# Top-k attention in two streams: the longest rows paired with the shortest

## The reference, cut to what matters

```python
dots = jnp.einsum('bhid,bhjd->bhij', q, k) * SCALE          # keys: 16 memory + n tokens
dots = jnp.einsum('bhij,hk->bkij', dots, pre_proj)          # heads are mixed
dots = jnp.where(causal, mask_value, dots)
kth = jax.lax.top_k(dots, TOPK)[0][..., -1:]                # TOPK = 64
dots = jnp.where(dots < kth, mask_value, dots)
attn = jax.nn.softmax(dots, axis=-1)
out = jnp.einsum('bhij,bhjd->bhid', attn, v)
return out.transpose(0, 2, 1, 3).reshape(b, n, H * DH) @ Wout + bout
```

## Time and profile before

| | |
|---|---|
| median of 3 runs | 5859.57 us (5858.61 to 5865.69) |
| profiled execution | 5879.23 us |
| its span | 5877.4 us, 141554 instructions |
| PE, PEld busy | 4961.7 us (84%), 3162.0 us (54%) |
| DVE busy | 4472.4 us (76%) |
| ACT, POOL busy | 3359.7 us (57%), 2310.0 us (39%) |
| mean granted clock of PE | 0.902 |

### The profile page before, as it was taken

How to read it: one execution, slowest core, us unless ns; L and a number is a source line. 1 busy time by engine, 2 the same in 40 slices (tenths; PEclk the granted TensorE clock), 3 DMA queues, 4 the chain that set the end, 5 groups by cost and what they waited for, 6 DMA issues and landing times. The chain is left out here.

```text
span 5877.4 us, 141554 instructions
## 1 busy us (share of the span) xinstructions
PE 4961.7 (84%) x53142; PEld 3162.0 (54%) x53334; DVE 4472.4 (76%) x8591; ACT 3359.7 (57%) x7309; POOL 2310.0 (39%) x3182
## 2 busy tenths in 40 slices
PE   4775999999999997667667677575999999999997
PEld 1322666666666665334334344343666666666665
DVE  5996777676767674898997997995777777777774
ACT  2433777676767675334334334332777777777775
POOL 1222666665666663000000000001666666666663
PEclk6998999999999999776877887776999999999998
DMA  0001222222222221000000000000222222222221
GB/s 17 0 0 36 66 73 66 71 65 72 64 74 63 74 63 29 16 1 2 1 2 2 1 1 1 1 2 25 68 70 71 70 66 74 63 74 67 74 66 37
DMA packets 162565, 248.01 MB, mean 42 GB/s; under 512 B 36228, under 2 KB 56640, under 8 KB 161734
## 3 DMA queue, kind: packets, MB, share of 16 engines
q1 hardware_dynamic: 161862, 238.65, 15.5%
HBM read 36.15 MB, written 1.05 MB: 6 GB/s over the span
## 5 line engine op out<-in xcount | busy, mean ns | idle before, releaser
L929 POOL TENSOR_TENSOR f_rope<-f_rope,f_t 128x1024 f32<-128x1024 f32 x384 | 906.4, 2360 | 475.2 <-DVE f_t L843 475.2
L942 POOL TENSOR_TENSOR f_rope<-f_rope,f_rn 128x1024 f32<-128x1024 f32 x384 | 731.3, 1904 | 59.9 <-POOL f_rn L921 4.4
L479 PE MATMUL psum<-f_wqkv,f_xs 128*128 128x512 f32 x1536 | 734.3, 601 | 17.0 <-DVE f_t L843 17.0
L848 DVE TENSOR_REDUCE f_ss<-f_sq 128x16 f32<-128x1024 f32 x384 | 466.1, 1214 | 336.8 <-ACT f_sq L710 333.4
L1722 DVE MAX8 tk_m<-tk_work 128x8 f32<-128x408 f32 (+28 forms) x1624 | 678.1, 460 | 0.0
L1761 POOL TENSOR_TENSOR X<-tk_y,X 128x128 f32<-128x128 f32 x16 | 7.0, 436 | 1674.1 <-ACT tk_y L1667 1674.1
L1727 DVE MATCH_REPLACE8 tk_work<-tk_m,tk_work 128x408 f32<-128x408 f32 (+28 forms) x1392 | 623.6, 456 | 0.0
L673 ACT ACTIVATE f_kT<-psum 64x512 f32<-64x512 f32 (+1 forms) x960 | 485.6, 525 | 81.6 <-PE psum L470 72.1
L710 ACT ACTIVATE f_sq<-psum 128x1024 f32<-128x1024 f32 x384 | 393.3, 1024 | 223.8 <-PE psum L479 223.3
L865 DVE TENSOR_REDUCE f_den<-f_prob 128x16 f32<-128x1024 f32 x192 | 234.2, 1220 | 365.4 <-ACT f_prob L715 365.4
L551 PE MATMUL psum<-f_wqkv,f_xs 128*128 128x512 f32 x768 | 383.3, 623 | 110.4 <-DMA f_wqkv<-in_Wqkv 75.7
(11 more groups left out here) (237 smaller groups left out, 10054.2 us busy)
## 6 DMA issues: line engine op xcount, KB each, us to landing
f_v<-f_v_tok SPq DMA_DIRECT2D x1152, 128.0 KB, 2.4
f_v<-f_v_tok SPq DMA_DIRECT2D x768, 64.0 KB, 2.0
f_wqkv<-in_Wqkv SPq DMA_DIRECT2D x36, 512.0 KB, 5.3
f_wo<-in_Wo SPq DMA_DIRECT2D x12, 512.0 KB, 4.3
f_w<-in_W SPq DMA_DIRECT2D x12, 341.0 KB, 4.0
f_w<-in_W SPq DMA_DIRECT2D x24, 64.0 KB
tk_wkv<-in_Wkv SPq DMA_DIRECT2D x1, 1024.0 KB
out<-y_tok SPq DMA_DIRECT2D x4, 256.0 KB, 2.5
```

The lines of the kernel that those rows point to most:

```text
L479: last = pe.matmul(psum[:, n, :], xs[:, j % 2, :], wqkv[:, INNER * which + 512 * n:INNER * which + 512 * (n + 1)], start=True, stop=True)
L848: dve.tensor_reduce(ss[:, H * half:H * (half + 1)], sq[:, half, :, :], AX_X, ALU.add).then_inc(s[f"{name}_ss"], 1)
L929: pool.tensor_tensor(part, part, t2[:, half, :, :], ALU.add).then_inc(s[f"{name}_added"], 1)
L942: pool.tensor_tensor(part, part, rn[:, H * half:H * (half + 1)].unsqueeze(2).to_broadcast([P, H, DH]), ALU.mult).then_inc(s[f"{name}_norme ...
```

## The change: what it does

`place` now alternates two streams: unit j = 0 of a pair walks down from the longest rows of the sequence, unit j = 1 walks up from the shortest. A pair is (63 - i, i) for i = 0 to 31. Its two units have 552 keys together, always. Four pairs make a *quad*: 32 neighbouring queries of each stream, so a block of `weigh` for each. The unit j = 1 of the first six pairs has at most 64 keys and one round, while its partner has eight: the number of rounds is now kept for each unit, with counters `found` and `gone` for the semaphore values.

What was done per tile is now done per quad or per two. `project_q` makes the queries of one quad, 32 of each stream: 16 products with 32 moving columns into one bank, in the first slot of the quad before. `weigh` of the long stream stands in the second slot of the next quad, of the short stream in the third, `turn_output` in the third and fourth. `output` is made per 64 queries and stream (two products, one after the other in the first slot of every second quad), and POOL adds halves of a tile. Values of the next sequence are made in slots 3 (two tiles), 4 (one) of that sequence and 23 (one) of the one before, keys in slots 3, 11, 19 and 27. The transposed probabilities lie in two buffers, for up to 3 full tiles and for 1.

```diff
 def place(unit):
     b, rest = divmod(unit, UNITS)
-    pos, u = divmod(rest, UNITS // TILES)
-    return b, TILES - 1 - pos, u
+    i, j = divmod(rest, 2)
+    g = i if j else UNITS - 1 - i
+    t, u = divmod(g, P // QB)
+    return b, t, u
...
+def values_due(slot):
+    b, at = divmod(slot, 4 * QUADS)
+    if 0 < b < B and at in (3, 4):
+        return [(b, t) for t in ((0, 1) if at == 3 else (2,))]
+    return [(b + 1, 3)] if at == 23 and b + 1 < B else []
+def halves_due(slot):
+    quad, r = divmod(slot, 4)
+    if r or quad % 2 == 0 or quad < 3:
+        return []
+    return [((quad - 3) // 2, stream) for stream in range(2)]
+def keys_due(slot):
+    b, at = divmod(slot, 4 * QUADS)
+    return [(b + 1, at // 8)] if at % 8 == 3 and b + 1 < B else []
+def queries_due(slot):
+    return [slot // 4 + 1] if slot % 4 == 0 and slot // 4 + 1 < QUADS * B else []
...
-def project_q(T):
-    b, t = tile(T)
-    for n in range(2):
-        bank = side(("q", T, n))
-        for c in range(4):
-            w0 = 512 * n + P * c
-            last = pe.matmul(bank[:, P * c:P * (c + 1)], wq[:, w0:w0 + P], k.XA[:, b, PAD + P * t:PAD + P * (t + 1)], start=True, stop=True)
-        last.then_inc(s["side_full"], 1)
+def project_q(quad):
+    bank = side(("q", quad))
+    for stream in range(2):
+        b, q0 = queries(quad, stream)
+        for c in range(PAIRS):
+            at = BLOCK * (PAIRS * stream + c)
+            last = pe.matmul(bank[:, at:at + BLOCK], wq[:, P * c:P * (c + 1)], k.XA[:, b, PAD + q0:PAD + q0 + BLOCK], start=True, stop=True)
+    last.then_inc(s["side_full"], 1)
...
-def output(T):
-    bank = side(("y", T))
-    pe.wait_ge(s["ot_evac"], 1 + 4 * T + 4)
+def output(h, stream):
+    bank = side(("y", h, stream))
+    pe.wait_ge(s["ot_evac"], 1 + 4 * h + 4)
     for c in range(8):
-        last = pe.matmul(bank[:, 0:P], wout[:, c // 4, c % 4, :], oT[:, c, :], start=(c == 0), stop=(c == 7))
+        last = pe.matmul(bank[:, 0:HALF], wout[:, c // 4, c % 4, :], oT[:, stream, c, :], start=(c == 0), stop=(c == 7))
...
 for slot in range(SLOTS + 5):        # PE
+    quad, r = divmod(slot, 4)
+    finished = 0 <= quad - 1 < QUADS * B
     if slot + 1 < SLOTS:
         raw_dots(slot + 1)
     if 0 <= slot - 1 < SLOTS:
         turn(slot - 1)
     if slot + 1 < SLOTS:
         mix(slot + 1)
-    if slot % 2 == 1 and 0 <= (slot - 3) // 2 < SLOTS // 2:
-        weigh((slot - 3) // 2)
-    if slot % 2 == 0 and 0 <= (slot - 4) // 2 < SLOTS // 2:
-        turn_output((slot - 4) // 2)
+    if finished and r in (2, 3):
+        turn_output(2 * (quad - 1) + r - 2)
+    if finished and r in (1, 2):
+        weigh(quad - 1, r - 1)
+    # then values, halves, keys and queries that are due in this slot; ACT copies in the same order
...
 def pair(p, between):                # DVE
-    rounds = ROUNDS if selects(2 * p) else 1
-    for r in range(rounds):
+    rounds = [ROUNDS if selects(2 * p + j) else 1 for j in range(2)]
+    for r in range(ROUNDS):
         for j in range(2):
+            if r < rounds[j]:        # maximum of unit j
...
         for j in range(2):
+            if r < rounds[j] - 1:    # strike of unit j
...
         if r == 5:
             between()                # now in all slots; reciprocal in slots 1 and 2 of a quad
```

More of the change, by code:

```diff
@@ L1340, in side_uses @@
-        return {use: i for i, use in enumerate(uses)}
[L1342 to L1352, removed]
+        for slot in range(SLOTS + 5):
+            uses += [("v", b, t, n) for b, t in values_due(slot) for n in range(2)]
+            uses += [("y", h, stream) for h, stream in halves_due(slot)]
+            uses += [("k", b, t, n) for b, t in keys_due(slot) for n in range(2)]
+            uses += [("q", quad) for quad in queries_due(slot)]
@@ L1354, in topk_phase, with queries, half_start @@
+        return {use: i for i, use in enumerate(uses)}
     AT = side_uses()
-    FIRST = 2 + 2 * TILES + 2 * TILES
+    FIRST = 1 + 2 * TILES + 2 * TILES
     def side_bank(i):
         return (SIDE, OUT, TURN_DIAG, TURN)[i % 4] if i < FIRST else SIDE
+    def queries(quad, stream):
+        b, t, u = place(8 * quad + stream)
+        return b, P * t + BLOCK * (u // 4)
+    def half_start(h, stream):
+        return h // 4, HALF * (h % 4 if stream else 7 - h % 4)
     with ExitStack() as ctx:
@@ L1469, in raw_dots @@
                 def raw_dots(pair):
[L1471 to L1474, removed]
+                    quad = pair // 4
+                    if pair % 4 == 0:
+                        pe.wait_ge(s["side_evac"], 1 + (1 + 2 * TILES if quad == 0 else AT[("q", quad)] + 1))
                     for j in range(2):
                         unit = 2 * pair + j
-                        u = place(unit)[2]
+                        b, t, u = place(unit)
                         if unit >= 2:
@@ L1593, in side, with copy_q @@
                     return psum[:, side_bank(i), :]
-                def copy_q(T):
-                    for n in range(2):
-                        bank = side(("q", T, n)).rearrange("p (g r u i) -> p g r u i", g=2, r=2, i=QB)
+                def copy_q(quad):
+                    bank = side(("q", quad)).rearrange("p (s g r u i) -> p s g r u i", s=2, g=4, r=2, i=QB)
+                    for stream in range(2):
                         for r in range(2):
@@ L1656, in normalise, with copy_output, copy_y @@
                     last.then_inc(s["o_done"], 1)
[L1658 to L1667, removed]
+                def copy_output(quad, stream):
+                    act.wait_ge(s["ot_full"], 1 + 2 * quad + stream + 1)
+                    b, q0 = queries(quad, stream)
+                    at = q0 % HALF
+                    copy(oT[:, stream, :, at:at + BLOCK], psum[:, OUT, 0:2 * P].rearrange("p (c q) -> p c q", q=BLOCK)).then_inc(s["ot_evac"], 1)
+                def copy_y(h, stream):
+                    bank = side(("y", h, stream))
+                    if h:
+                        act.wait_ge(s["added"], 1 + 2 * h + stream - 1)
+                    act.activation(y[:, stream, :], bank[:, 0:HALF], ACT.Identity, bias=bout[:, 0:1]).then_inc(s["side_evac"], 1)
                 copy_q(0)
@@ L1676, in _ @@
                 for slot in range(SLOTS + 5):
-                    T, part = divmod(slot, TILE_PAIRS)
+                    quad, r = divmod(slot, 4)
+                    finished = 0 <= quad - 1 < QUADS * B
                     if slot + 1 < SLOTS:
@@ L1685, in _ @@
                         copy_scores(slot + 1)
[L1686 to L1693, removed]
-                    if part == 5 and T + 1 < B * TILES:
-                        copy_q(T + 1)
-                    if slot % 2 == 1 and 0 <= (slot - 3) // 2 < SLOTS // 2:
-                        normalise((slot - 3) // 2)
+                    if finished and r in (2, 3):
+                        copy_output(quad - 1, r - 2)
+                    for b, t in values_due(slot):
+                        copy_v(b, t)
+                    for h, stream in halves_due(slot):
+                        copy_y(h, stream)
+                    for b, t in keys_due(slot):
+                        copy_k(b, t)
+                    for next_quad in queries_due(slot):
+                        copy_q(next_quad)
+                    if finished and r in (1, 2):
+                        normalise(2 * (quad - 1) + r - 1)
             @block.vector
@@ L1735, in pair @@
                             between()
-                    if rounds == 1:
-                        between()
-                    else:
-                        for j in range(2):
-                            dve.wait_ge(s["m8"], 1 + count["m8"] - 1 + j)
+                    for j in range(2):
+                        if rounds[j] > 1:
+                            dve.wait_ge(s["m8"], 1 + found[j])
                             dve.wait_ge(s["e_done"], 1 + 2 * p + j + 1)
@@ L1746, in between @@
                     def between():
[L1747 to L1748 removed]
+                        quad, r = divmod(slot, 4)
+                        if 0 <= quad - 1 < QUADS * B and r in (1, 2):
+                            recip(2 * (quad - 1) + r - 1)
                     if slot < SLOTS:
```

132 lines of the change are left out of this document (63 added, 69 removed).

## The result

The changed kernel takes 5958.6 us (median of 4 runs, 5946.5 to 5966.2) against 5860.2 of the kernel before (4 runs, 5858.6 to 5865.7): a ratio of 1.0164, interval 1.0143 to 1.0186. It is slower, by 98 us. Its profiled execution took 5966.17 us, span 5964.3: 87 us over the span before. The other 11 us of the difference lie between single executions.

The account below looks back on a forecast made before the run. VectorE was taken to bound long rows, the round TensorE, ScalarE, TensorE short ones. Pairing -112.7, one stream +35, tail +9 and stalls +85 gave +16 on 5859.6: 5876 us; range 5803 to almost 5969.

Parts of the forecast that it names:

- rival B3: Query and output products: narrow ones cost what wide ones do, through weight loads; net +109 us, 5969 us; chance 0.13.
- the mechanism held to be likeliest: Selecting phase: TensorE at a mixed clock, stalls between all-high and all-low cases; 5876 us, own range 5855 to 5915; chance 0.45.
- Pairing, -112.7: Selecting phase: pairs of 552 columns take 12.3 us each and all of VectorE's idle time, 112.7 us, goes.
- One stream alone, +35: 24 slots whose short unit needs one maximum: the long stream's dependent steps lose 0.11 us each; +35 us, bounds 0 and 45.
- The tail, +9: After VectorE's last selection: two weighings in turn and two output products follow; +9 us, bounds +5 and +12.
- Stalls, 85: VectorE waiting for late TensorE work within slots: 85 us, taken between 68 (lengths halfway) and 125 (mean of the ends).
- A: Turn of a batch, 3 times: value and key banks make TensorE late; stalls sum to 12 or 81 us, 46 halfway.
- B: Quad with output product, 12 times: stall 0 at high clock or 10.2 us at low (122 in all), 22 halfway.
- C: Quad without output product, 15 times: stall 0 at high clock or 2.3 us at low (35 in all), 0 halfway.
- I take the middle, 2.2 and 4.2: Bank of 32 narrow query records: 2.2 us at 2.4 GHz, 4.2 at 1.2 GHz, between a quarter and all of the 128-column rate.
- 1.7 and 2.7: Each 64-column output product with its copy: 1.7 us at 2.4 GHz, 2.7 at 1.2 GHz.
- The allowance of 17 for steady lateness: In the stall term: 85 us taken over the 68 of halfway lengths, since lateness counts while earliness is lost.

Follow-up runs that it names:

- The experiment with all rounds: Fastest kernel (merged products, late reciprocal, spread side work) with all eight rounds and the final selection for units of at most 64 keys too: 5826.7 us, 0.9935.

## Why the forecast came out as it did

The direction was right and 5958.6 lies in the range, some 10 us under its upper end. The likeliest time, 5876, was 83 us low. The range held because it reached almost to rival B3's 5969; the mechanism held to be likeliest gave 5855 to 5915 and missed, so the hit is in part luck. By its own steps:

*Pairing, -112.7.* Right. A full slot without a stall is 12.26 to 12.35 us where 12.3 was worked out, no slot behind the start waits for scores, and no other idle time remains than between the steps of the lone stream and at the reciprocal. ACT ended 0.2 us of waits behind the start. (The regular falls of DVE that the prediction read from the earlier trace rows are one to 8 and two to 7, not four to 7; nothing in its sum rests on that.)

*One stream alone, +35.* Measured 28.7 more of busy time and 10.6 of idle between the steps, 39.3. Such a slot without a stall takes 11.6 to 12.5 us where about 11.5 was worked out. The experiment with all rounds bears on it: filling the pauses doesn't win them back.

*The tail, +9.* Measured +12.7, just over its bound of +12. The two output products, 8.5 us with their copies and the last addition where the one before took 4.7, add 3.8 for the 1.2 that was put in, and that is most of it.

*Stalls, 85.* This step failed, with 146.7. The places were right, the sizes not: slot 5 42.3 for the 46 of A; slots 13, 21 and 29 79.4 for the 22 of B; the others 25.0 for the 0 of C. The cause of what B and C lacked is the term "I take the middle, 2.2 and 4.2" for a bank of queries, which measured 3.76 and 7.04, and "1.7 and 2.7" for an output product, which measured 2.0 + 0.4 and 3.67 + 0.4. The term's bounds were a quarter and all of the price of 128 columns, and nearly all of it was right. That is rival B3's mechanism, and B3's 89 in B and +109 in all stand beside 79.4 and the span's +87. It had been given 0.13. By the rule of the Trainium skill that was weighed ("TensorE: Matmul & The Clock Gate", section "LDWEIGHTS (loading the stationary operand)"), the queries would be 3.4 us, an estimate. At the high level the trace is near it, with 3.76. At the low level it is not, with 7.04: the skill's figure names no level.

The second thing that the term left out is the level. Lengths were set halfway between the two; the query records were at the low one in 873 of 992 intervals. The kernel with wide query products separates the two: 45 us of stalls went with the level, as the price of a record at either level did not change. The allowance of 17 for steady lateness stood for this and was too small. C's small stalls fit a bank of queries 1.6 to 2.8 us dearer. A came out near its 46 although the dearer banks should have raised it (B3 had 17 more), so another part of it was sized too large. One part is seen: its sums had the scores of slot 4 come late as well (8.0 us at the low level), and no slot waited for them. The rest was not tried.

With measured sizes the sum is -112.7 + 39.3 + 12.7 + 146.7 = +86.0, and the span gives +86.9. The rest is the phase's later start, 2.7, less the 1.8 behind the tail. From the first query record to the first maximum there are 22.4 us where there were 16.7. Of the 5.7 more, the first bank of queries makes 3.3 (7.01 us for 3.75) and the first keys 2.2 (9.92 for 7.75, with the same 64 records); the stages before ended 3.0 earlier. The 11 us by which medians differ more than the profiled spans are not explained.

The signs that were named: DVE busy 1557.9 for 1564, with 1880 maxima as before; gaps of 0.03 us in the 24 slots, where about 0.1 was named; the idle time named as foreseen and mostly at the foreseen slots; records 0.112 us apart at the high level, where 0.1 or more was to prove B3; tail 25.4 for some 22.

## What to carry to other kernels

Before cutting a product into narrower ones, count its records and weight loads: with 128x128 weights, 32 columns cost what 128 do, so blocks that share weights belong in one product over a strided operand, or the cut undoes what the better balance wins (+98 us turned into -23 by that alone, and into -51 with a later wait and spread side work). When an engine is filled to its limit, a wait in the middle of its stream becomes a deadline for the others: put it as late as its consumer allows. It was worth 68 and 24 us in two streams and nothing clear in the old order. And the idle time that a new pairing removes was also slack for side work, which now makes stalls where it piles up. Spreading it anew took the worst pile away, but by itself was worth no more than 4 us here, which the noise may hold.

## What was not expected of the hardware

Query products with 3.6 times the moving columns made the kernel 42 us faster, with the mean granted clock from 2390 to 3900 us at 0.79 in place of 0.77: PE was "busy" with 32-column products and at 1.2 GHz for most of them, and with 128-column ones it was more often at 2.4. The spacing of the records shows it bank by bank. Of the 32 banks of 32-column products 22 were at 1.2 GHz from end to end, 8 began at 2.4 and fell inside the bank, 2 stayed at 2.4, and in none did the clock rise. With 128 columns it rose to 2.4 inside 28 banks, in 3 of them after a fall, and was there throughout in the other 4. Dependence between VectorE's steps costs about 0.11 us each, 39 us over 24 slots, against two independent streams in turn.
